# A planned order for a fused attention and feed-forward block: later weight loads moved among SyncE's copies, and the order of all engines written anew

## The reference

```
qkv = einsum('bnd,ed->bne', x, qkv_w) + qkv_b        # split per head into q, k, v
attn = softmax(einsum('bhqd,bhkd->bhqk', q, k) * 8 ** -0.5)
out = einsum('bhqk,bhkd->bhqd', attn, v)             # heads put back side by side
x = layernorm(x + out @ fc_w.T + fc_b + x)
h = silu(x @ w1.T * w1_s) * (x @ w2.T * w2_s)        # 512 wide
h = gelu(h @ h1.T * h1_s)                            # 512 x 512
h = gelu(h @ h2.T * h2_s)                            # 512 x 512
x = layernorm(x + h @ w3.T * w3_s)
```

## Time and profile before

| | |
|---|---|
| time before, median of 3 runs | 312.81 us (312.67 to 313.73) |
| the profiled execution | 313.6 us, of it 311.8 us span of the trace |
| PE busy | 290.1 us (93%) |
| DVE busy | 249.6 us (80%) |
| ACT busy | 241.4 us (77%) |
| POOL busy | 143.4 us (46%) |
| DMA queue of SP | 15.22 MB, 24.9% of 16 engines' span |

### The profile page before, as it was taken

How to read it: one execution, slowest core, us unless ns; L and a number is a source line. 1 busy time by engine, 2 the same in 40 slices (tenths; PEclk the granted TensorE clock), 3 DMA queues, 4 the chain that set the end, 5 groups by cost and what they waited for, 6 DMA issues and landing times.

```text
span 311.8 us, 6746 instructions
## 1 busy us (share of the span) xinstructions
PE 290.1 (93%) x2337; PEld 167.9 (54%) x2337; DVE 249.6 (80%) x561; ACT 241.4 (77%) x458; POOL 143.4 (46%) x255
## 2 busy tenths in 40 slices
PE   8959699999999999999999999998999999999991
PEld 8733254456555546353444363454556568558980
DVE  0669779998989999798899868538998784658993
ACT  2744588898979998999999888989886896984440
POOL 5162679514628991606149816707493290000101
PEclk9979899999999999999999999999999999999996
DMA  5687410045641004403610034450100000010011
GB/s 156 192 149 166 151 37 5 4 65 72 107 68 35 4 0 69 71 5 47 93 52 4 2 55 85 67 78 10 34 4 3 2 3 2 2 36 0 3 34 38
DMA packets 20276, 15.67 MB, mean 50 GB/s; under 512 B 2945, under 2 KB 19090, under 8 KB 20242
## 3 DMA queue, kind: packets, MB, share of 16 engines
q1 hardware_dynamic: 20242, 15.22, 24.9%
HBM read 5.51 MB, written 1.05 MB: 21 GB/s over the span
## 4 chain that ended last, share of the span: by engine, by line
PE 65%; DVE 12%; ACT 8%; SPq 5%; issue 4%; DMA 3%; POOL 0%; POOLq 0%; DVEq 0%; ACTq 0%
PE bank L484 23%; PE bank L524 14%; PE bank L495 8%; PE bank L506 8%; DVE negmax L879 7%; SPq L382 4%; ACT prob L735 4%; PE bank L466 2%; PE bank L548 2%; DMA stack<-mT 2%; PE bank L477 2%; DMA stack<-parts 1%; PE bank L578 1%; PE bank L459 1%; PE bank L565 1%
## 5 line engine op out<-in xcount | busy, mean ns | idle before, releaser
L879 DVE TENSOR_REDUCE negmax<-bank 128x1 f32<-128x512 f32 x256 | 159.8, 682 | 29.9 <-PE bank L495 29.4
L735 ACT ACTIVATE prob<-bank 128x512 f32<-128x512 f32 x256 | 134.0, 618 | 9.1 <-PE bank L506 8.0
L484 PE MATMUL bank<-act,hT 128*128 128x256 f32 (+1 forms) x384 | 71.0, 329 | 0.3 <-DVE negmax L879 0.2
L524 PE MATMUL bank<-prob,v_sb 128*32 128x256 f32 (+1 forms) x768 | 67.4, 458 | 1.2 <-DVE negmax L879 0.9
L484 PEld LDWEIGHTS bank<-act,hT 128*128 128x128 f32 x384 | 55.2, 189 | 11.6 <-issue 3.7
L495 PE MATMUL bank<-stack 64*128 64x512 bf16 x256 | 56.8, 385 | 4.5 <-DMA stack<-parts 3.2
L506 PE MATMUL bank<-stack 64*128 64x256 bf16 (+1 forms) x384 | 55.1, 309 | 3.6 <-DMA stack<-mT 2.8
L802 ACT ACTIVATE h_nat<-bank,hs_all 128x256 f32<-128x256 f32 (+1 forms) x48 | 25.0, 548 | 20.2 <-PE bank L484 19.9
L506 PEld LDWEIGHTS bank<-stack 64*128 64x128 bf16 x384 | 19.6, 94 | 32.1 <-issue 13.5
L524 PEld LDWEIGHTS bank<-prob,v_sb 128*32 128x32 f32 x768 | 21.7, 109 | 26.9 <-issue 16.9
L495 PEld LDWEIGHTS bank<-stack 64*128 64x128 bf16 x256 | 15.9, 94 | 34.3 <-issue 19.7
(11 more groups left out here) (119 smaller groups left out, 357.3 us busy)
## 6 DMA issues: line engine op xcount, KB each, us to landing
stack<-parts SPq DMA_DIRECT2D x64, 128.0 KB, 3.9
x_in<-in_L_attn_x_dram SPq DMA_DIRECT2D x4, 256.0 KB, 3.5
h_nat<-in_L_ffn_h_w_dram SPq DMA_DIRECT2D x1, 1024.0 KB, 7.8
work<-in_L_ffn_h_w_dram SPq DMA_DIRECT2D x1, 1024.0 KB, 6.3
res<-in_L_attn_x_dram SPq DMA_DIRECT2D x4, 256.0 KB, 3.4
work<-in_L_ffn_w_w_dram SPq DMA_DIRECT2D x2, 256.0 KB, 3.4
out_dram<-y SPq DMA_DIRECT2D x4, 128.0 KB, 2.9
out_dram<-y SPq DMA_DIRECT2D x2, 256.0 KB, 2.3
```

The lines of the kernel that those rows point to most:

```text
L484: mm = nc.tensor.matmul(dst, w, v, start=first and n == 0, stop=last and n == len(pairs) - 1)
L524: last = nc.tensor.matmul(space("P", pfirst)[at:at + VW, 0:w], v_sb[b % 2][:, kt, of:of + VW], prob[:, t % NP, c * w:(c + 1) * w], start=k ...
L735: nc.scalar.activation(prob[:, n % NP, :], space("T", n)[:, :], ACT.Exp, scale=SCALE).then_inc(emptied("T", n), 1)
L879: nc.vector.tensor_reduce(negmax[:, g % 2, col:col + 1], space("S", n)[:, :], AX.X, ALU.max, negate=True).then_inc(emptied("S", n), 1)
```

## The change

No arithmetic is added or taken away, and both kernels have the same 256 `S`, `T` and `e`, the same 180 `H`, 30 `K` and 18 table loads on ACT. The table `NORM` leaves all normalizing on DVE, where it was. What changes is the order. Of the strings one line is shown, the beginning of SP's:

```diff
 SP_ORDER = """
 lw lh xin vb
-zk zq zk zq*4 zk*6 mrow zq*3 l3 lh mrow xres mrow more xin mrow*2 spread mrow spread*2 xin spread mrow xres mrow*2 spread*2 mrow*2 spread*2 mrow xres
...
+zk*2 zq*2 zk zq zk zq*3 zk*4 zq*2 mrow lh mrow more mrow xin l3 xres mrow*2 spread*2 mrow spread mrow spread xin mrow xres spread mrow spread mrow
...
-    LN_STEPS = 5
+    LN_STEPS = 4
...
+    NORM = [(1, 1), (1, 1), (1, 1), (1, 1), (1, 1), (1, 1)]
...
-        x1_ok, y_ok = sem("x1_ok"), sem("y_ok")
+        x1_ok, y_ok = ([sem(f"{n}{e}") for e in range(2)] for n in ("x1_ok", "y_ok"))
...
+        def normalize(eng, do, e, i, n):
+
+            u = ON_N[i][e][n]
+            b, t0, nt = UNITS[u]
+            eng.wait_ge(rs_ok[i], u + 1)
+            if i:
+                wait(eng, st_out, 16 * BEFORE[u])
+            elif b > 1:
+                eng.wait_ge(ps_x1T, LAST[b - 2] + 1)
+                until_empty(eng, "Y", LAST[b - 2])
+            dst, done = ((x1[b % 2], x1_ok), (y, y_ok))[i]
+            for t in range(t0, t0 + nt):
+                last = do.tensor_scalar(dst[:, t, :], res[i][:, t, :], mv[i][:, t, 0:1], rstd[i][:, 1, t:t + 1], ALU.subtract, ALU.mult)
+            last.then_inc(done[e], 1)
```

More of the change, by code:

```diff
@@ L9 @@
 lw lh xin vb
[L10 to L11 removed]
+zk*2 zq*2 zk zq zk zq*3 zk*4 zq*2 mrow lh mrow more mrow xin l3 xres mrow*2 spread*2 mrow spread mrow spread xin mrow xres spread mrow spread mrow
+spread mrow spread mrow xres mrow spread*2 out*2 mrow spread*2 mrow xres mrow*3 out*4"""
 PE_ORDER = """
[L14 removed]
@@ L141, in post_ln_block_kernel @@
     GATE_VEC = [(u, k) for u in range(NU) if u in GATE_DVE for k in range(NK)]
+    ON_N = [[[u for u in range(NU) if NORM[u][i] == e] for e in range(2)] for i in range(2)]
     ON_0 = [[(u, k) for u in range(NU) for k in range(NK) if SPLIT0[u] == e] for e in range(2)]
@@ L445, in _ @@
                     sp.wait_ge(ps_wq, 2)
-                    wait(sp, x1_ok, FIRST[n])
+                    if n:
+                        until_norm(sp, 0, FIRST[n] - 1)
                     sp.dma_start(x_res[:, :, :], x[n].rearrange("(t p) c -> p t c", p=P)).then_inc(ld_res, 16)
@@ L845, in layernorm @@
                     dve.wait_ge(ps_w3T, u + 1)
-                    wait(dve, y_ok, BEFORE[u])
+                    if BEFORE[u]:
+                        until_norm(dve, 1, BEFORE[u] - 1)
                     nc.vector.tensor_tensor(flat(r), space("Y", u)[:, 0:width(u)], flat(x1_b), ALU.add).then_inc(emptied("Y", u), 1)
@@ L857, in layernorm @@
                     last.then_inc(ln_step[i], 1)
-                elif k == 3:
+                else:
                     dve.wait_ge(ln_step[i], 3 * u + 2)
                     nc.vector.tensor_scalar(rstd[i][:, 0, tiles(u)], mv[i][:, tiles(u), 1], EPS, None, ALU.add).then_inc(ln_step[i], 1)
-                else:
-                    dve.wait_ge(rs_ok[i], u + 1)
-                    if i:
-                        wait(dve, st_out, 16 * BEFORE[u])
-                    elif b > 1:
-                        dve.wait_ge(ps_x1T, LAST[b - 2] + 1)
-                    dst, done = ((x1_b, x1_ok), (y, y_ok))[i]
-                    for t in ts:
-                        last = nc.vector.tensor_scalar(dst[:, t, :], r[:, t, :], mv[i][:, t, 0:1], rstd[i][:, 1, t:t + 1],
-                                                       ALU.subtract, ALU.mult)
-                    last.then_inc(done, 1)
             for what, n, _ in walk(DVE_ORDER):
@@ L928, in _ @@
                     last.then_inc(emptied("o", n), 1)
+                elif what in ("n1", "n2"):
+                    normalize(dve, nc.vector, 1, int(what == "n2"), n)
                 elif what in ("l1", "l2"):
@@ L1002, in _ @@
                         nc.gpsimd.memset(mhalf[:, :], -0.5).then_inc(vzero, 1)
+                elif what in ("n1", "n2"):
+                    normalize(pool, nc.gpsimd, 0, int(what == "n2"), n)
                 elif what in ("p1", "p2"):
```

78 lines of the change are left out of this document (41 added, 37 removed).

## The result

The changed kernel takes 315.53 us (median of 6 runs, 314.50 to 316.46), the kernel before 313.55 us beside it (6 runs, 312.67 to 314.53). The ratio is 1.0064, 95% interval 1.0035 to 1.0093: slower by 2 us and clear of noise, where 3.1 us less were forecast. The profiled execution took 315.5 us, of it 313.6 us span.

What follows compares the result with a forecast made beforehand. Three engines carry loads of the same order, none the bound throughout. Gains of 1.2 + 1.0 + 0.9 = 3.1 us, everything else at zero, gave 309.7 us against 312.81, range 306.3 to 314.6.

Steps and rivals of the forecast that it cites:

- Everything else: Order between 40 and 280 us, new tokens, outputs of units 0 and 1: costed at zero, 2.5 us either side.
- Term 1, the start: First 40 us: reordered copies and spreads fill DVE's idle holes; 1.2 us gained, bounds -0.5 and 2.7.
- Term 2, the spreads: Last batch, around 180 us: earlier split shrinks DVE's 2.51 us hole; 1.0 us gained, bounds 0 and 2.5.
- the second rival: Start and spreads give nothing: 1 MB load lands later, PE bounds 200 to 210 us; 311.9 us, chance 0.25.
- Term 3, the end: Three `W` and a `Y` moved behind the last `H`, into a wait; 0.9 us gained, bounds -0.5 and 1.26.
- The third: Rival: ACT becomes the bound, 32 exponentials in place of 25 behind the last reduction; slower, 315.4 us, chance 0.20.
- The clock: Low clock at 38 to 40 us may go, worth up to 1 us, counted in the start's upper bound.
- The first stretch: Low granted clock (0.50) from 20 to 22 us, after PE's gap around 16 to 19 us: should stay.

Runs made afterwards that it cites:

- the pair with both operations halved: The good order and the changed kernel, each with row maxima and exponentials over 256 of 512 columns: 305.87 and 306.28 us.
- the two pairs with one halved: The good order and the changed kernel with half exponentials: 309.78 and 313.25 us; with half row maxima: 308.85 and 313.31 us.
- the moved `P`: The good order with 41 `P` in PE's order moved behind up to two, four or six following score tiles: 325.31, 334.05 and 346.57 us.
- the good order: The changed kernel's code with its new order up to the 56th `S` (about 56 us), the order of before behind it: 310.15 us, ratio 0.9896.
- the run on term 3: The good order with only the changed kernel's end on PE, DVE and ACT: 311.65 us, ratio 0.9922.
- the run on term 2: The good order with DVE's last Q and K split five reductions earlier and two `S` ahead of five `H` pieces: 315.38 us, ratio 1.0042.
- the run up to the 96th `S`: The changed kernel's order on all engines up to the 96th `S` (95 us), the order of before behind it: 315.64 us, ratio 1.0055.

## Why the prediction was wrong

The forecast was 309.7 us, and it is 315.5.

**Everything else, 0 with 2.5 to either side: the step that failed.** I wrote that "it is the same work by the same engines", and I looked only for copies that come late. The stretch from 59 to 261 us lost 7.1 us in place of 0, and 60 to 180 us alone 5.0 (-4.64 to +0.36), which the forecast itself named as what would refute it. In place of that step the runs showed: the same work in another order waits longer for PSUM banks, 12.1 us in place of 4.9, because a tile's turn on PE comes before DVE or ACT has emptied its bank. It is shown by the pair with both operations halved, where the difference of the whole times falls from 5.4 to 0.4 us and that of this stretch from 7.0 to 2.6, as the waits do. That it is DVE and ACT by turns, and not one of them, is shown by the two pairs with one halved. Which of the five orders makes the waits (PE's, or those by which DVE and ACT come to empty) was not parted: they changed together. That PE's order alone can cost as much is shown by the moved `P`, but there late results of `P` hold ACT and DVE too.

**Term 1, the start, 1.2 (bounds -0.5 and 2.7).** The direction was right, the size not: 3.4 us to the end by the run with the new start alone. What I missed is the row on fillers. I read "PE is idle for up to a quarter of that time; nothing waits for it then" and costed it at zero; in fact `x` waited for PE's zeros, and four `K` fewer are worth 1.3 us. All later times of the term are early, by that for the most part: I had the fifth `T` at 35.0 to 35.8, it stands at 33.15. That DVE's hole would fall below 1 us held (0.48), and that the second row copy no longer holds anything too: it is issued at 29.56 us (forecast: after 31), and its semaphore is full at 31.83, within 2.3 us of the issue and 0.16 behind the landing of the 1 MB load at 31.67. It still lands right behind the load; the load was only down earlier than I had it (33.6). The remaining 2.1 us are DVE's holes and the stretches at 1.2 GHz, which no run took apart.

**Term 2, the spreads, 1.0 (0 to 2.5).** Worth nothing. From the 183rd to the 215th `S` the changed kernel takes 33.77 us, the good order 33.42 and the kernel before 33.45, though the chain there leads through no spread any more, as forecast. The hole of 2.51 us became one of 1.14 and, further on, this one in the timeline of DVE, in front of the row of `H` that I had mentioned:

```profile
191.69 0.69 DVE L894 TENSOR_REDUCE negmax<-bank 128x1 f32<-128x512 f32 x1 [1.14 <-PE bank L503]
213.65 1.29 DVE L894 TENSOR_REDUCE negmax<-bank 128x1 f32<-128x512 f32 x2 [9.30 <-PE bank L503]
```

9.30 us of idle time cost nothing, since PE is full there: the second rival had that. Alone and without its surroundings the move even costs 4 us.

**Term 3, the end, 0.9 (-0.5 to 1.26).** Right in the changed kernel, a little too large: the last `H` ends 0.7 us earlier, measured from the last exponential, and DVE's last step 0.6 us (29.46 for 30.10). The 33.48 against 33.60 us to the end hide it, since the last `out` lands 0.54 us later after that step. On the old rest the same end gave nothing (30.14), so the gain hangs on what stands ahead of it, which my sum, two durations taken off a chain, did not have.

**The rivals.** The third gave 315.4, and its sign came true: the last reduction is not earlier (254.67 for 254.86), and the exponentials end 1.9 us later, where it had 3.5. But its mechanism is not what the runs show: with exponentials of half the size the changed kernel is still 3.5 us behind. It names one of the two engines between which the wait changes hands. So that the number came true was luck: it was put together from other terms than those measured, 4.6 won at the start, 7.1 lost in the middle, 1.3 won behind it and 0.5 given back by the landing of `out`. That ACT's exponentials behind the last reduction are the price was argued and not shown.

**The clock.** Granted clock 1.00 at 38 to 40 us came as said. The first stretch did not stay in this execution, but it does in others of the same start: in the run on term 3 the windows are

```profile
20.00:22.00 2.00, 1.53 (x10) 0.72 (x11) 1.79 (x4) 1.16 (x3) 0.55 (x3) 0.50 0.71 159
22.00:24.00 2.00, 1.93 (x8) 0.49 (x5) 2.00 (x4) 0.06 (x1) 1.72 (x6) 0.50 0.85 172
```

and its 49th `S` starts at 48.68 us, 0.27 later than in the run without it. The cost varies: of the runs with whole operations and this start, the four at 1.00 throughout have that tile at 47.82 to 48.52 us, and the four others with a low stretch or two ahead of it at 49.30 to 50.13. So the first stretch can stay, as I had it; it comes and goes between executions of one start, and is worth 0.2 to 2 us (an estimate from these times). Part of the new start's gain may be that.

**What stays open.** Why the order of the changed kernel has more such waits, as one number that could be read from an order ahead of a run, was not found: long rows are not it. Which engine's order makes them is open too. Whether another order of PE alone would win the 7 us back in the changed kernel was not tried.

## What to carry to other kernels

When every engine's order is new, "same work, same busy time" is no reason for zero: cost the stretch between the visible edits by how each matmul finds its output bank, and leave it a range of some per cent of its length (here 7 us of 195). An engine can be the one that all wait through without being the one that is too slow: test by shortening both partners of a shared buffer at once, since with one shortened the other takes its place. And zeros that keep PE busy stand in order like any work: look at what has already landed when the last of them ends.

## What the runs showed of the hardware

- The page's busy share of PE hides waits of up to 0.8 us between matmuls; they are seen as idle time of PEld with a releaser. The Trainium skill (Perfetto Trace Analysis, Identifying the Most-Contended Engine) says that matmul busy time is no good measure of how close TensorE is to its best and points to the busy share of weight loads; for the first the trace agrees, with 93% in kernels of 305.87 and 315.53 us. The share of weight loads tells them apart no better (54% and 53%); their idle time by releaser does.
- Two score tiles on different halves of the 128 partitions start at the same moment (0.00 us apart), pairs follow each other after 0.21 to 0.22 us. The Trainium skill (TensorEngine Tiling (Array Packing), PSUM Bottleneck) warns that tiling speeds up TensorE and not the emptying of PSUM; by it the trace agrees, with 0.11 us for a tile on PE against 0.60 for DVE (thirteen in 7.85 us) and 0.50 for ACT.
- A stretch of 2 us in the middle of the kernel in which PE is busy for 0.56 or 0.67 us was followed by a granted clock of 0.65 and 0.63 in the next 2 us and of 0.50 for 2 and 4 us behind them (from 176 us in the run on term 2, from 96 us in the run up to the 96th `S`).
- DVE's operation on two SBUF operands took 1.28 us for two alone and 2.61 beside POOL's, and POOL's own 1.72 in place of 1.28.
- The last copy of the output, which stands last among SP's in all orders, lands 2.3 to 4.3 us after DVE's last step. Comparisons of the end should stop at that step.
